# Gathering 56 of 88 groups of edge features beside the edge matrices, with the ids decoded ahead of them

## The reference

```python
edge_index = jnp.stack([src, dst])
x = _layernorm(x + _L0_gnn_ref(x, wc, wn, bias, edge_index))            # alpha + mean of beta[dst] over src + bias
x = _layernorm(x + _L1_gnn_ref(x, edge_index, Wq, ...))                 # two attention layers over the edges
x = _layernorm(x + _L2_gnn_ref(x, edge_index, edge_weight, W, b))       # normalised, weighted sum over edges
x = _layernorm(x + _L3_gnn_ref(x, edge_index, edge_attr_128, ...))      # messages with edge features
...
# inside the last part: the only place that reads the 128 features of each edge
edge_emb = edge_attr @ W_edge + b_edge
msg = relu(node_feats[src] + edge_emb)
aggr = segment_sum(msg, dst, num_segments=N)
```

## Time and profile before

| | |
|---|---|
| median of 3 runs | 2711.61 us (2704.99 to 2712.08) |
| profiled execution | 2706.75 us, its span 2705.0 us |
| PE busy | 2453.5 us, 91% of the span |
| DVE busy | 2075.7 us, 77% |
| ACT busy | 1663.4 us, 61% |
| POOL busy | 1034.5 us, 38% |
| feature gathers (L761) | 352, 342.8 us busy, mean 974 ns; 369.1 us idle before them, 282.9 of it for the store of a group |

### The profile page before, as it was taken

How to read it: one execution, slowest core, us unless ns; L and a number is a source line. 1 busy time by engine, 2 the same in 40 slices (tenths; PEclk the granted TensorE clock), 3 DMA queues, 4 the chain that set the end, 5 groups by cost and what they waited for, 6 DMA issues and landing times. The chain is left out here.

```text
span 2705.0 us, 44125 instructions
## 1 busy us (share of the span) xinstructions
PE 2453.5 (91%) x12631; PEld 1914.2 (71%) x12631; DVE 2075.7 (77%) x4118; ACT 1663.4 (61%) x3700; POOL 1034.5 (38%) x1030
## 2 busy tenths in 40 slices
PE   5999799999799999997899998688999999986887
PEld 3677555555487999856799996346777777765766
DVE  8698899998535888835388885566899999966667
ACT  1489888883224777712277773141899999935560
POOL 1777000004103444450045454322777777710211
PEclk9999899999898999998999999899999999988989
DMA  2040000004243444222443432412877777831101
GB/s 91 2 123 3 11 0 0 0 0 140 99 162 95 112 114 114 68 93 90 147 110 102 117 105 62 118 49 97 248 241 236 238 239 237 215 72 51 63 4 43
DMA packets 116592, 278.09 MB, mean 103 GB/s; under 512 B 24039, under 2 KB 38314, under 8 KB 116462
## 3 DMA queue, kind: packets, MB, share of 16 engines
q0 software_dynamic: 51328, 138.78, 18.9%
q1 hardware_dynamic: 65134, 137.65, 16.2%
HBM read 208.80 MB, written 59.43 MB: 99 GB/s over the span
## 5 line engine op out<-in xcount | busy, mean ns | idle before, releaser
L761 POOL DMA_INDIRECT feature_rows<-in_edge_attr,ids x352 | 342.8, 974 | 369.1 <-DMA features_dram<-feature_rows 282.9
L1879 POOL DMA_INDIRECT x_got<-table_dram,src_idx x352 | 375.3, 1066 | 110.0 <-issue 81.7
L1312 DVE TENSOR_TENSOR pt_low<-bank,pt_high 128x640 fp32r<-128x640 f32 x320 | 262.9, 822 | 53.5 <-ACT pt_high L1275 52.2
L713 ACT ACTIVATE hot_rest<-hot_dst,slot_w 128x128 bf16<-128x128 bf16 x864 | 272.9, 399 | 40.7 <-DVE hot_dst L663 40.7
L1275 ACT CAST pt_high<-bank 128x640 fp32r<-128x640 f32 x320 | 219.6, 687 | 115.7 <-PE bank L1226 115.6
L2023 DVE TENSOR_TENSOR msg<-bank,x_got 128x512 f32<-128x512 f32 x352 | 237.0, 684 | 41.9 <-ACT msg_high L1968 15.0
L764 POOL COPY ids<-id_idx 128x32 uint32<-128x32 uint32 (+1 forms) x5 | 1.2, 240 | 651.7 <-DVE id_idx L874 338.6
L1306 DVE CUSTOM_DVE_ANT_0 p<-bank,log_counts 128x1254 f32<-128x1254 f32 x160 | 232.7, 1454 | 14.1 <-PE bank L1209 14.0
L1226 PE MATMUL bank<-ident,p 128*128 128x128 f32 x1600 | 229.0, 275 | 2.3 <-DVE pt_low L1312 2.3
L1267 ACT ACTIVATE p<-p,bound 128x1254 f32<-128x1254 f32 x160 | 215.3, 1346 | 9.0 <-DVE bound L1306 9.0
L1237 PE MATMUL bank<-pt_high,val 128*128 128x256 f32 x800 | 213.1, 301 | 0.9 <-DVE agg_t L1318 0.9
(11 more groups left out here) (417 smaller groups left out, 6331.4 us busy)
## 6 DMA issues: line engine op xcount, KB each, us to landing
features_dram<-feature_rows POOLq DMA_DIRECT2D x88, 256.0 KB, 2.4
edge_got<-features_dram SPq DMA_DIRECT2D x88, 256.0 KB, 4.1
qk_dram<-qk_high SPq DMA_DIRECT2D x16, 640.0 KB, 2.9
qk_dram<-qk_low SPq DMA_DIRECT2D x16, 640.0 KB, 4.2
keys<-qk_dram SPq DMA_DIRECT2D x32, 320.0 KB, 4.7
queries<-qk_dram SPq DMA_DIRECT2D x32, 320.0 KB, 6.7
queries_low<-qk_dram SPq DMA_DIRECT2D x32, 320.0 KB, 8.7
acc_a<-zeros SPq DMA_DIRECT2D x1, 6400.0 KB
```

What stands on the lines that cost most here:

```text
L713: last = act.activation(hot_rest[:, u, j, q, :], hot_dst[:, u, :, j], ACT.Copy, scale=k.slot_w[:, 1 + q, bass.ds(tile0 + j, 1)])
L761: pool.indirect_dma_start(out=rows[:, g % 2, j * ED:(j + 1) * ED], out_offset=None, in_=self.a.edge_attr_128, in_offset=bass.IndirectOffse ...
L1312: dve.tensor_tensor(p_low[:, made % 3, :, columns], unit(2 * n + u).rearrange("p (j n) -> p j n", n=P), p_high[:, made % 3, :, columns].bi ...
L1879: pool.indirect_dma_start(out=xg[:, g % XRING, j, :], out_offset=None, in_=k.table_dram, in_offset=bass.IndirectOffsetOnAxis(ap=k.src_idx[ ...
```

## The change

The body for POOL and the decoding of the ids move from `layer0` to `edge_matrices`. There DVE decodes first and builds its first hot matrix afterwards; POOL waits for the ids and gathers 56 groups (FIRST_GROUPS = 88 - 2 * 16). LAYER_GROUPS becomes 16 and ATTEND_GROUPS 8, so that each `attend` gathers 8 groups instead of 32, and each `finish_layer` 8 as before. In `layer0` DVE's ten instructions and the wait behind them are gone, and POOL has no body. The tiles for ids and rows now lie behind those of `edge_matrices`.

```diff
-def edge_matrices(nc, k):
+def edge_matrices(nc, k, features):
...
+    ids_made = S("ids_made")
+    dst_part, bits, number = r.take("dst_part", [P, NT], I32), r.take("part_bits", [P, 4, NT], I32), r.take("part_numbers", [P, 3, NT], F32)
+    features.places(r, "0", FIRST_GROUPS)
     with nc.Block() as block:
+        @block.gpsimd
+        def _(pool):
+            pool.wait_ge(ids_made, 1)
+            features.gather(pool, 0, FIRST_GROUPS, 1)
+
         @block.vector
...
+            me = Steps(nc, dve, "numbers_dve")
+            id_part = k.id_idx[:].bitcast(I32)
+            me.then(dve.tensor_copy(dst_part[:], k.slot_dst[:]))
+            for q, (part, op, n) in enumerate(((dst_part, ALU.bitwise_and, 255), (dst_part, ALU.arith_shift_right, 8),
+                                               (id_part, ALU.arith_shift_right, 9), (id_part, ALU.bitwise_and, 511))):
+                me.mark(dve.tensor_scalar(bits[:, q, :], part[:], n, None, op))
...
+            dve.tensor_copy(k.id_idx[:], number[:, 2, :]).then_inc(ids_made, 1)
 
             dve.sem_inc(added, 4)
             load(NPAIR // 2)
...
-LAYER_GROUPS = 40
-ATTEND_GROUPS = 32
+LAYER_GROUPS = 16
+ATTEND_GROUPS = 8
...
-def layer0(nc, k, features):
+def layer0(nc, k):
...
-        @block.gpsimd
-        def _(pool):
-            pool.wait_ge(ids_made, 1)
-            features.gather(pool, 0, FIRST_GROUPS, 1)
-
...
-            id_part = k.id_idx[:].bitcast(I32)
-            me.then(dve.tensor_copy(dst_part[:], k.slot_dst[:]))
...
-            dve.tensor_copy(k.id_idx[:], number[:, 2, :]).then_inc(ids_made, 1)
-            dve.wait_ge(ids_made, 1)
-
```

More of the change, by code:

```diff
@@ L685, in add_second @@
                 add(g, 1, ((word >> 9) & 15).with_bounds(min_val=0, max_val=NB - 1), ((word >> 7) & 3).with_bounds(min_val=0, max_val=2), following)
+            me = Steps(nc, dve, "numbers_dve")
[4 more added lines that the diff above has]
+                me.mark(dve.tensor_scalar(bits[:, q, :], part[:], n, None, op))
+            dve.wait_ge(me.sem, me.n)
+            me.mark(dve.tensor_copy(k.slot_dst[:], bits[:, 0, :]))
+            me.then(dve.tensor_copy(number[:], bits[:, 1:4, :]))
+            me.then(dve.scalar_tensor_tensor(number[:, 1, :], number[:, 0, :], 8.0, number[:, 1, :], ALU.mult, ALU.add))
+            me.then(dve.scalar_tensor_tensor(number[:, 2, :], number[:, 1, :], float(EC), number[:, 2, :], ALU.mult, ALU.add))
+            dve.tensor_copy(k.id_idx[:], number[:, 2, :]).then_inc(ids_made, 1)
             dve.sem_inc(added, 4)
@@ L788, in layer0 @@
     var_ready, dev_ready, x1_ready, x1_stored = S("var0_ready"), S("dev0_ready"), S("x1_ready"), S("x1_stored")
-    x1t_done, x1t_copied, ids_made = S("x1t_transposed"), S("x1t_copied"), S("ids_made")
+    x1t_done, x1t_copied = S("x1t_transposed"), S("x1t_copied")
     counts_above, logs_made, logs_masked = S("counts_above"), S("logs_made"), S("logs_masked")
@@ L798, in layer0 @@
     of_source, above = r.take("of_source", [P, NP], F32), r.take("counts_above", [P, 2, NP], F32)
-    features.places(Region(nc, k.rec_at, k.beta_end), "0", FIRST_GROUPS)
-    r = Region(nc, ARENA_END - 4 * 3 * NP, ARENA_END)
-    dst_part, bits, number = r.take("dst_part", [P, NT], I32), r.take("part_bits", [P, 4, NT], I32), r.take("part_numbers", [P, 3, NT], F32)
     y = k.alpha
     with nc.Block() as block:
-        @block.gpsimd
-        def _(pool):
-            pool.wait_ge(ids_made, 1)
-            features.gather(pool, 0, FIRST_GROUPS, 1)
         @block.tensor
@@ L2559, in program @@
     sort_edges(nc, k, a)
-    edge_matrices(nc, k)
-    layer0(nc, k, features)
+    edge_matrices(nc, k, features)
+    layer0(nc, k)
     nc.clear_and_free_semaphores(nc.allocated_since(used_by_edges))
```

## The result

The changed kernel takes 2863.2 us (median of 4 runs, 2860.93 to 2866.24), the kernel before beside it 2711.85: ratio 1.0568, 95% interval 1.0554 to 1.0582. Two later sets gave 1.0566 and 1.0561. The forecast was 2859 us, its range 2838 to 2895.

The account below looks back on a forecast made before the run. DVE bounds the edge matrices, TensorE layer 0 and attention; after the change POOL ends the edge-matrix block. 146.6 + 3 + 0 = 149.6 us on 2706.75 gives 2856.4; halfway between two bases 2859 us, range 2838 to 2895.

Parts of the forecast that it names:

- The step that carried it: Edge-matrix block: POOL's 56 groups end after DVE and the barrier holds all engines; layer 0 starts 146.6 us later.
- third rival: End of the edge-matrix block: nobody waits for POOL's last groups, attention is relieved, 2683 us; chance 0.03.
- decoding, DVE: Start of the edge-matrix stage: DVE's work ends 4.0 us later, and nothing comes back in layer 0.
- pace beside DVE: Edge-matrix block: POOL takes 8.2 us a group while DVE works, bounds 7.87 and 9.93.
- cold PE: Start of layer 0: TensorE, after standing some 140 us, runs at a lower clock and adds 3 us.
- attention, 24 groups less: Attention stages: 24 groups fewer in each give back 0, bounds -5 us a layer and 0.
- The mis-sized term: End of the edge-matrix block: the barrier after POOL's last store takes 1.0 us.
- The squared-length estimate: Edge-matrix block: a gather waits for the one running DVE operation, 0.08 us a gather, 0.33 us a group.
- The first rival: Edge-matrix block: whole runs of DVE's short operations lock POOL out, pace 9.75 or more, about 2903 us; chance 0.09.
- The second rival: Edge-matrix block: DVE waits for a whole gather each time, 217 us on DVE, about 2931 us; chance 0.03.
- the threshold: Edge-matrix block: 56 groups fit the room only at 5.5 us a group.
- One sign: Attention stages: POOL done after 8 groups, some 65 to 75 us in.

Follow-up runs that it names:

- g1_after: The changed kernel again, unaltered, against the kernel before: 2861.6 us, ratio 1.0566.
- i1_after: The changed kernel once more, unaltered, in a later set, against the kernel before: 2862.2 us, ratio 1.0561.
- g2_eight: The changed kernel with 8 groups beside the edge matrices and 40 in each layer, ids still decoded ahead: 2712.5 us, ratio 1.0016 to the kernel before.
- h1_ring: The changed kernel with four row buffers, gathers two groups ahead of the store: 2730.5 us, ratio 1.0076 to the kernel before; 1.0816 in the set at 3019 us.
- e6_split: The changed kernel with 36 groups beside the edge matrices, 12 in layer 0's block and 20 in each layer: 2716.8 us, ratio 1.0036 to the kernel before.
- h2_fortyeight: The changed kernel with 48 groups beside the edge matrices and 20 in each layer: 2796.1 us, ratio 1.0321 to the kernel before.

## Why the prediction was right

The step that carried it held: the block ends with POOL, and the barrier passes that on in full (third rival: out; layer 0 waited 148 us, and attention gave nothing). Term by term, in the changed kernel's profile:

| step | forecast | measured |
|---|---|---|
| decoding, DVE | 4.0 us, ids at 302.3 | 298.40 to 302.37, POOL's copy at 302.44 |
| first store | 10.9 later, 313.2 | 11.2 later, 313.6 |
| pace beside DVE | 8.2 (7.87 to 9.93) | 8.20 over 37 steps |
| pace after it | 7.87 | 8.03 over 17 steps |
| end of DVE's stage | 614.9 | 616.1 |
| last store landed | 756.5 | about 759.1 |
| barrier | 1.0 | 5.4, of it POOL's DRAIN 5.13 |
| layer 0 starts | 757.5 | 764.5 |
| cold PE | +3 in layer 0 | 119.8 us of layer 0, 116.8 before: +3.0 |
| attention, 24 groups less | 0 a layer (-5 to 0) | 305.8 against 306: 0 |

**The mis-sized term** is the barrier. I took 1.0 us from the earlier trace rows, where PE stands 1.05 us, but there DVE is last, whose DRAIN takes 0.60 us; POOL, which had no work in that block, was no guide. When POOL is last, its DRAIN is exposed. The trace before had such DRAINs too, hidden: 3.33 us behind the 8 groups of layer 0 and 4.29 behind the 32 of an attention stage. They would have given 3 to 4 us instead of 1.0. The barrier is 4.4 of the 7.0 us by which layer 0 started later than forecast. The other 2.6 are the pace after DVE's end: its steps were not all 7.9, one of them 8.99 (a gather stood 1.40 us instead of 0.30 before it could issue) and one 9.24 (a store took 3.93 us to be seen instead of 2.6). On the mean step that is 8.03 against 7.87, 2.7 us over the 17 steps; a first store 0.4 late and an end 0.7 shorter than forecast nearly cancel.

The total came out closer than its terms. They add up to 149.6 us, and the profile has 152.6 for layer 0's start (153.6 less the 1.0 by which the sort ended later) and 3.0 in layer 0, 155.6. The medians differ by 151.4, 154.0 and 153.8 us in three sets. That 2859 lies only 4 us below 2863.2 owes something to the scatter of the first set.

**The price of DVE beside the gathers.** The squared-length estimate gave 0.33 us a group, and 8.20 against 7.87 looks like that number, but part of it is luck. The 37 steps beside DVE hold two long ones, 9.31 and 9.73 us, the 25th and 36th. Two more, the 43rd and 51st, come after DVE's end, and g1_after and i1_after have long steps at the same four places, which speaks against DVE as their cause. Without them it is 8.13 against 7.88: 0.25 us a group. The gathers of the changed kernel issued beside DVE, and behind it (303 to 616 us, 617 to 760 us; min/median/max ns):

```profile
L782 POOL DMA_INDIRECT feature_rows<-in_edge_attr,ids x155: 943/968/1248, 303.7 to 614.9; - x155
```

```profile
L782 POOL DMA_INDIRECT feature_rows<-in_edge_attr,ids x69: 943/947/973, 616.2 to 752.6; - x69
```

The median is 21 ns longer, the longest 0.3 us, the mean 56 ns (1010 against 954 ns), where the estimate said 80. The estimate also left out, without a reason, DVE's two adds of 0.59 us in each turn; with them it would have said about 0.18 us a gather (an estimate from the starts 400.78, 401.34 and 401.85 of a turn in this trace), three times what came. That it is DVE's turn that stretches them shows in their ends: of 34 gathers of 1.05 us or more between 306 and 610 us, 23 end 0.41 to 0.45 us after the start of an add on `acc_c`; of the 116 shorter ones at most 6 do.

The first rival (whole runs lock POOL out) needed a pace of 9.75; it is out. Of the lock rule of the Trainium skill ("SBUF — State Buffer", section "SBUF: two separate sides") no more than this shows beside operations this short, and nothing like the fivefold time in the page's own case of a copy. The second rival (DVE waits for a gather each time) needed 217 us on DVE. From its first hot matrix to its last operation's end DVE took 313.1 us (303.02 to 616.09) against 312.3 before (298.34 to 610.59): 0.8 us. Where POOL doesn't hide it, with 36 groups, it is no larger.

**The decoding** was rightly priced at its full 4.0: g2_eight, which pays it alone, is 4.9 us above the kernel before on the medians, and its block is 4.5 us longer. Nothing came back in layer 0, which takes 116.9 us with and without it.

**On the threshold** the prediction named 5.5 us a group. The ring came to 5.7, with a first store 5 us later, and missed it by a little, and e6_split met it with fewer groups. Both did what the change set out to do, and neither gained. That part was in the prediction only as a zero, and it is the more useful result: room on an idle engine is worth nothing for work that nobody waits for where it is.

**One sign was off.** POOL was to be done 65 to 75 us into each attention stage; its last store had landed 82 us into the first (997.6 to 1080.0), with one store seen only after 10.16 us. Nobody waited for it. The steps beside DVE, 7.89 to 9.73 us, stayed within the bounds named.

In the set at 3019 us two of my steps would have been wrong, DVE beside gathers and the zero of attention, though the changed kernel itself wasn't run there. The profile before, taken in other conditions, holds nothing that tells of them.

## What to carry to other kernels

Before moving work into an engine's idle time, multiply the count by the serial step of that work (here 8 us a group, most of it gathers plus the round trip of a store) and compare it with the room: 54 steps were 440 us in a stage of 313, and a barrier made all of the rest everybody's. Then ask what the work costs where it stands; a copy of the kernel that leaves it out tells it in one run, and here the answer was nothing. A block that ends with POOL also pays POOL's DRAIN, so read that row in blocks where it is hidden.

## What the runs showed of the hardware

- POOL's DRAIN at the end of a block of gathers depends on the number of groups in it, but not steadily. It took 3.31 to 3.33 us after 8 groups, 4.94 after 12 and 7.39 to 7.40 after 18; 4.29 after 32 and 5.95 after 36; 1.86 after 48 and 5.13 after 56. So it grows by 0.41 us a group and falls back by about 9 us (an estimate from that slope) somewhere between 18 and 32 groups and again between 36 and 48. Each value is the same within 0.03 us wherever that number of groups was gathered with two buffers, in the set at 3019 us too; the ring's 56 groups had 7.17. What makes it fall back is open. DVE's DRAIN at the end of the edge matrices was 0.60 each time. Two of POOL's rows, of h2_fortyeight and e6_split:

```profile
L646 POOLq DRAIN  x1: 1863/1863/1863, 691.7 to 691.7; - x1
```

```profile
L646 POOLq DRAIN  x1: 5947/5947/5947, 595.0 to 595.0; - x1
```

- The granted clock was 0.51 in the 148 us in which PE stood, TensorE's 1.2 GHz level, and the first 40 transposes behind them took 7.19 us. After a stop of 1.05 us 20 took 2.37. Layer 0 as a whole took 119.8 to 119.9 us after stops of 18, 80 and 148 us alike (h1_ring, h2_fortyeight, the changed kernel) and 116.8 to 116.9 without one. The granted clock of its first 17 to 18 us was 0.83 after 18 us of stop, 0.85 after 148 and 1.00 in the kernel before.
- POOL's gathers beside DVE's turns are stretched at fixed points of the turn, by 56 ns in the mean; DVE isn't slowed by more than 0.8 us in 313.
- One program can run in conditions where each stage with software-issued DMAs is longer while those without are not: the sort's scatters took 374 us instead of 204 and the kernel 3019 instead of 2708. A ratio measured there (1.08 for the ring) says nothing of the other conditions (1.008).
